# Queries and keys turned by crossbar DMA transposes in a macaron block's attention

## The reference

```python
x = x + 0.5 * ffn(layernorm(x)); x = x + attn(layernorm(x)); x = x + 0.5 * ffn(layernorm(x))

def attn(x):                                   # B, T, C = 8, 512, 128; H, D = 16, 64
    q, k, v = [(x @ W).reshape(B, T, H, D) for W in (Wq, Wk, Wv)]
    q, k = rmsnorm(q, q_rms_w), rmsnorm(k, k_rms_w)        # over D, times a weight for each channel
    gate = softplus(einsum('bthd,hd->bht', k, u_n) / sqrt(D))
    bias = -dist * omega_eff[h] * gate[b, h, j]            # dist = max(i - j, 0), -inf above the diagonal
    attn = softmax(einsum('bihd,bjhd->bhij', q, k) / sqrt(D) + bias)
    return einsum('bhij,bjhd->bihd', attn, v).reshape(B, T, H * D) @ Wproj
```

## Time and profile before

| | us |
|---|---|
| median of 3 runs (lowest, highest) | 913.05 (911.69, 913.4) |
| the profiled execution | 911.52 |
| its span, first to last instruction | 909.7 |
| one round in the middle of it | 102.9 |

### The profile page before, as it was taken

How to read it: one execution, slowest core, us unless ns; L and a number is a source line. 1 busy time by engine, 2 the same in 40 slices (tenths; PEclk the granted TensorE clock), 3 DMA queues, 4 the chain that set the end, 5 groups by cost and what they waited for, 6 DMA issues and landing times.

```text
span 909.7 us, 26061 instructions
## 1 busy us (share of the span) xinstructions
PE 836.1 (92%) x10168; PEld 614.0 (67%) x10168; DVE 691.9 (76%) x1724; ACT 640.0 (70%) x1384; POOL 593.9 (65%) x708
## 2 busy tenths in 40 slices
PE   4648898999999999999999999999999999999984
PEld 2234766578677676777677776777677776777773
DVE  7648776888879887788868888788868888688432
ACT  4645758776877769776877769776877769784633
POOL 3632667577678667687578667687478667686662
PEclk8778999999999999999999999999999999999997
DMA  7033321534051600524052600624042600605000
GB/s 198 4 70 83 84 59 29 114 69 87 2 123 43 142 1 23 133 62 94 2 111 47 152 1 11 146 60 96 2 103 52 151 6 1 153 23 122 3 14 12
DMA packets 28962, 61.18 MB, mean 67 GB/s; under 512 B 5398, under 2 KB 15848, under 8 KB 28776
## 3 DMA queue, kind: packets, MB, share of 16 engines
q1 hardware_dynamic: 28840, 59.52, 29.1%
HBM read 5.29 MB, written 2.10 MB: 8 GB/s over the span
## 4 chain that ended last, share of the span: by engine, by line
PE 69%; DVE 12%; ACT 9%; POOL 5%; issue 4%; SPq 1%; DMA 0%; POOLq 0%; ACTq 0%; DVEq 0%
PE ps L749 12%; PE ps L751 11%; PE ps L750 11%; PE ps L845 6%; PE ps L860 6%; PE ps L887 6%; PE ps L888 6%; DVE negm L1117 4%; POOL pt_l L573 3%; PE ps L775 3%; PE ps L757 3%; PE ps L889 2%; PE ps L861 2%; ACT sq L667 2%; ACT qkn L668 2%
## 5 line engine op out<-in xcount | busy, mean ns | idle before, releaser
L573 POOL TENSOR_TENSOR pt_l<-pt 128x512 f16<-128x512 f32 (+1 forms) x384 | 332.7, 899 | 139.1 <-ACT pt L725 138.5
L1117 DVE TENSOR_REDUCE negm<-ps 128x1 f16<-128x512 f32 (+3 forms) x512 | 213.1, 485 | 22.9 <-PE ps L861 22.4
L725 ACT ACTIVATE pt<-ps 128x512 f32<-128x512 f32 (+1 forms) x384 | 177.5, 533 | 54.8 <-PE ps L889 42.8
L591 POOL TENSOR_TENSOR qkn<-qkn,rs 128x512 f32<-128x512 f32 x128 | 132.6, 1067 | 85.4 <-ACT rs L678 85.4
L887 PE MATMUL ps<-q,k 128*128 128x512 f16 (+3 forms) x512 | 146.7, 299 | 1.1 <-ACT pt L725 1.1
L888 PE MATMUL ps<-q,k 128*128 128x512 f16 (+3 forms) x512 | 146.5, 299 | 0.0
L749 PE MATMUL ps<-v_buf,pt 128*128 128x65 f16 x1280 | 129.6, 194 | 8.6 <-DVE ytok L1135 6.7
L860 PE MATMUL ps<-k,q 96*128 96x512 f16 (+3 forms) x512 | 121.7, 307 | 14.4 <-DMA k<-gtt 7.5
L749 PEld LDWEIGHTS ps<-v_buf,pt 128*128 128x128 bf16 x1280 | 118.1, 98 | 18.0 <-issue 13.0
L750 PE MATMUL ps<-v_buf,pt 128*128 128x65 f16 x1280 | 129.8, 193 | 0.0
L751 PE MATMUL ps<-v_buf,pt_l 128*128 128x65 f16 x1280 | 129.6, 193 | 0.0
(11 more groups left out here) (174 smaller groups left out, 2076.1 us busy)
## 6 DMA issues: line engine op xcount, KB each, us to landing
q<-qkn SPq DMA_DIRECT2D x96, 256.0 KB, 4.9
k<-qkn SPq DMA_DIRECT2D x96, 256.0 KB, 5.7
x_in<-in_L_attn_x SPq DMA_DIRECT2D x8, 256.0 KB, 3.1
out<-x_out SPq DMA_DIRECT2D x8, 256.0 KB, 6.4
k<-q SPq DMA_DIRECT2D x1, 1024.0 KB, 10.4
k<-gtt SPq DMA_DIRECT2D x64, 8.0 KB
sq<-in_L_ffn_W SPq DMA_DIRECT2D x2, 256.0 KB
q<-in_L_attn_Wq SPq DMA_DIRECT2D x1, 512.0 KB, 4.7
```

Of the source, the lines that this page charges most:

```text
L573: g.tensor_tensor(pt_l[:, h % 2, c], pt[:, h % 2, c], pt_h[:, h % 2, c], ALU.subtract).then_inc(s_pt_l, 1)
L591: g.tensor_tensor(qk, qk, r.unsqueeze(3).broadcast_to([P, HH // 2, 2, D]), ALU.mult).then_inc(s_qkn, 1)
L725: a.activation(pt[:, h % 2, c], ps[:, j, 0:width], ACT.Exp).then_inc(s_exp, 1)
L1117: ins = d.tensor_reduce(negm[:, ib, row(h):row(h) + 1], part.bank(s, i)[:, col:col + (ib + 1) * P], AX.X, ALU.max, negate=True)
```

## The change

Queries and keys stay with tokens on partitions through the norm and the split. ACT copies them from PSUM into `qkf` (two buffers by token block), POOL multiplies both by the inverse root and the queries once more by a row `qkw` = query weight x key weight / 8, so that the keys need no weight. In the step `tr` (half, token block), which replaces `t`, ACT writes the high part into `qkt`, DVE the low part beside it (both read SBUF), and SP issues two DMA transposes of 128 x 1024 16-bit elements, `qkt` to `k2` and to `q2`. `rows` is then two copies of 64 partitions x 8 heads x 512 tokens, from `q2` and `k2` to `q1` and `k1`, and the four rows of gates. A half thus has 8 transposes of 256 KB and 2 copies of 512 KB. Heads lie in `q1`, `k1`, `q2`, `k2` in their own order, and `row()` and its like are gone. The weights are first loaded into `pt`, `pt_l` and `q2` in place of `q2` and `k2`. The tables `PART` are written anew.

```diff
 PART = {
...
     "body": [
...
-        ("s", 9, THIS), ("gl", 0, NEXT), ("t", 0, NEXT), ("t", 1, NEXT), ("gate", 0, NEXT), ("pv", 8, THIS),
-        ("t", 2, NEXT), ("t", 3, NEXT),
-        ("s", 10, THIS), ("gr", 0, NEXT), ("pl", 9, THIS), ("pl", 10, THIS), ("rows", 0, NEXT), ("yt", 3, THIS),
...
+        ("s", 15, THIS), ("tr", 1, 0, NEXT), ("tr", 1, 1, NEXT), ("qk", 1, 2, NEXT), ("pl", 14, THIS),
+        ("qkn", 1, 2, NEXT), ("a", 5, NEXT), ("qk", 1, 3, NEXT), ("a", 6, NEXT), ("a", 7, NEXT), ("pv", 14, THIS),
+        ("nm", 0, NEXT), ("qkn", 1, 3, NEXT), ("pl", 15, THIS), ("tr", 1, 2, NEXT), ("wp", 2, THIS), ("gl", 1, NEXT),
+        ("tr", 1, 3, NEXT), ("yt", 6, THIS), ("gate", 1, NEXT), ("v", 0, 3, NEXT),
...
-UNITS = {"m": 2, "h": 4, "out": 1, "qk": 2, "gl": 1, "gr": 1, "t": 2, "a": 3, "nm": 1, "v": 1, "yt": 1, "wp": 1}
+UNITS = {"m": 2, "h": 4, "out": 1, "qk": 2, "gl": 1, "gr": 1, "a": 3, "nm": 1, "v": 1, "yt": 1, "wp": 1}
...
-        qkn = sb("qkn", [P, 2, 2, HH // 2, T // 2])
+        qkf = sb("qkf", [P, 2, 2, HH * D])
+        qkt = sb("qkt", [P, 2, 2, HH, 2, D], F16)
...
+            def turn_operands(part, s, b, hf, t):
+
+                blk = (b * 2 + hf) * TB + t
+                if b > 0 and t == 0:
+                    sp.wait_ge(s_s_ps, ((b - 1) * H + (hf + 1) * HH) * 3)
+                for n, (j, dst) in enumerate(((1, k2), (0, q2))):
+                    sp.wait_ge(s_lo, blk * 2 + n + 1)
+                    sp.dma_start_transpose(dst[:, hf * HH:(hf + 1) * HH, t * P:(t + 1) * P],
+                                           qkt[:, t % 2, j, :, :, :].rearrange("p h a n -> p (h a n)")).then_inc(s_turned[t % 2], 16)
+
             def place_operands(part, s, b, hf):
 
-                def place(dst, j, lo, done):
-                    for n in range(2):
-                        sp.dma_start(dst[:, (2 * hf + n) * HH // 2:(2 * hf + n + 1) * HH // 2, :],
-                                     qkn16[n * D:(n + 1) * D, j, lo, :, :]).then_inc(done, 16)
-
-                sp.wait_ge(s_hi, b * H + (hf + 1) * HH)
-                place(q1[0:D, :, :], 0, 0, s_grow)
-                place(k1[0:D, :, :], 1, 0, s_grow)
+                hs = slice(hf * HH, (hf + 1) * HH)
+                for i in range(2):
+                    sp.wait_ge(s_turned[i], (b * 2 + hf + 1) * TB * 16)
+                sp.dma_start(q1[0:D, hs, :], q2[0:D, hs, :]).then_inc(s_grow, 16)
+                sp.dma_start(k1[0:D, hs, :], k2[D:P, hs, :]).then_inc(s_grow, 16)
                 part.taken(sp, ("gr", *s[1:]))
                 for r in range(4):
-                    sp.dma_start(k1[GROW + r:GROW + r + 1, hf * HH:(hf + 1) * HH, :],
-                                 gtt[r * HH:(r + 1) * HH, :]).then_inc(s_grow, 16)
-                place(q2[0:D, :, :], 0, 0, s_dup)
-                place(k2[D:P, :, :], 1, 0, s_dup)
-                part.taken(sp, ("t", 4 * hf + 3, s[-1]), 1)
-                place(q2[D:P, :, :], 0, 1, s_low)
-                place(k2[0:D, :, :], 1, 1, s_low)
+                    sp.dma_start(k1[GROW + r:GROW + r + 1, hs, :], gtt[r * HH:(r + 1) * HH, :]).then_inc(s_grow, 16)
...
             def over_rms(part, s, b, hf, t):
-                pool.wait_ge(s_rs, (b * 2 + hf) * TB + t + 1)
-                for j in range(2):
-                    qk = qkn[:, j, t // 2, :, (t % 2) * P:(t % 2 + 1) * P].rearrange("p i (h n) -> p i h n", n=D)
-                    r = in_rows(rs[:, t, j * HH:(j + 1) * HH])
-                    g.tensor_tensor(qk, qk, r.unsqueeze(3).broadcast_to([P, HH // 2, 2, D]), ALU.mult).then_inc(s_qkn, 1)
+                blk = (b * 2 + hf) * TB + t
+                pool.wait_ge(s_rs, blk + 1)
+                heads = [qkf[:, t % 2, j, :].rearrange("p (h n) -> p h n", n=D) for j in range(2)]
+                r = [rs[:, t, j * HH:(j + 1) * HH].unsqueeze(2).broadcast_to([P, HH, D]) for j in range(2)]
+                g.tensor_tensor(heads[0], heads[0], r[0], ALU.mult).then_inc(s_qn, 1)
+                g.tensor_tensor(heads[1], heads[1], r[1], ALU.mult).then_inc(s_kn, 1)
...
+                g.tensor_tensor(heads[0], heads[0], qkw[:, :].unsqueeze(1).broadcast_to([P, HH, D]), ALU.mult).then_inc(s_qnw, 1)
...
+                    if blk >= 2:
+                        act.wait_ge(s_lo, (blk - 2) * 2 + 2 - j)
+                    part.taken_by(a.activation(qkf[:, t % 2, j, :], part.bank(s, j), ACT.Copy, scale=1.0 / QKV_UP), s, j)
+
+            def hi_parts(part, s, b, hf, t):
+
+                blk = (b * 2 + hf) * TB + t
+                if blk >= 2:
+                    act.wait_ge(s_turned[t % 2], (blk // 2) * 32)
+                for j in (1, 0):
+                    act.wait_ge(s_kn if j else s_qnw, blk + 1)
+                    a.activation(qkt[:, t % 2, j, :, j, :], qkf[:, t % 2, j, :].rearrange("p (h n) -> p h n", n=D),
+                                 ACT.Copy).then_inc(s_hi, 1)
...
-            def turn_heads(part, s, b, p):
-
-                pe.wait_ge(s_qkn, (b * 2 + p // 4 + 1) * TB * 2)
-                for j in range(2):
-                    part.room(pe, s, j)
-                    for t in range(TB):
-                        mm = pe.transpose(part.bank(s, j)[:, t * P:(t + 1) * P],
-                                          qkn[:, j, t // 2, p % 4, (t % 2) * P:(t % 2 + 1) * P], ident[:, :])
-                    part.filled_by(mm, s, j)
...
+            def lo_parts(part, s, b, hf, t):
+                blk = (b * 2 + hf) * TB + t
+                for n, j in enumerate((1, 0)):
+                    dve.wait_ge(s_hi, blk * 2 + n + 1)
+                    d.tensor_tensor(qkt[:, t % 2, j, :, 1 - j, :], qkf[:, t % 2, j, :].rearrange("p (h n) -> p h n", n=D),
+                                    qkt[:, t % 2, j, :, j, :], ALU.subtract).then_inc(s_lo, 1)
```

More of the change, by code:

```diff
@@ L140, in units_of @@
     return UNITS.get(s[0], 0)
-def units(part):
-    return sum(units_of(s) for s in PART[part])
 def slopes_of(heads):
@@ L348, in macaron @@
         s_out = sem("s_out")
-        s_dup = sem("s_dup")
-        s_low = sem("s_low")
+        s_turned = [sem(f"s_turned{i}") for i in range(2)]
         s_grow = sem("s_grow")
@@ L378, in macaron @@
         s_hi = sem("s_hi")
+        s_lo = sem("s_lo")
+        s_qkw = sem("s_qkw")
         s_s_ps = sem("s_s_ps")
@@ L700, in gate_softplus @@
                 a.activation(lgl[:, :, :], lge[:, :, :], ACT.Ln, bias=1.0).then_inc(s_lgl, 1)
-            def hi_parts(part, s, b, p):
-                if b == 0 and p == 0:
-                    act.wait_ge(s_prepared, 1)
-                for j, w in enumerate((qws, kws)):
-                    part.full(act, s, j)
-                    a.activation(qkn16[:, j, 0, p % 4, :], part.bank(s, j), ACT.Identity, scale=w[:, :]).then_inc(s_hi, 1)
             def v_hi(part, s, b, j, t):
```

328 lines of the change are left out of this document (146 added, 182 removed).

## The result

| | before | after |
|---|---|---|
| median of 4 runs each (lowest, highest), us | 913.04 (911.69, 913.4) | 989.05 (987.96, 994.29) |
| span of the profiled execution, us | 909.7 | 992.4 |
| a round in the middle, us | 102.9 | 116.0 |

The ratio is 1.084, with a 95% interval of 1.080 to 1.089. The forecast was 882 us, and its range ended at 940: wrong in sign, and the time lies above that of every rival too (974 at most).

A forecast was written before the change was run, and what follows sets the result against it. PE was taken as the bound, busy 101.1 of 102.9 us a round. Seven rounds 4.9 us shorter and a lead 3 us longer gave 911.5 - 7 x 4.9 + 3 = 880.2, so 882 us at the median; range 857 to 940.

The forecast's parts named there:

- coupling cost: In a round, PE waiting through the two-buffer chain of ACT, DVE and POOL: 3.1 us, between 0 and 8.
- The gain on PE: In a round, PE's turns (line 845) go: 8.0 us less, from readings of 8.8 and 7.2, leaving 93.1 us of work.
- The sum's "7 x": Seven rounds between 104.7 and 825 us, each taken as 4.9 us shorter (98.0 instead of 102.9).
- DVE's low parts: On DVE, 16 a round at 0.69 us by length plus 0.5 waiting beside POOL; DVE at 90.8 us a round.
- POOL's sum: POOL from 72.5 to 89.0 us a round: 8 more operations at 1.06 us, and waits of 16 x 0.5.
- ACT: ACT's 16 high parts a round at 0.63 instead of 0.70 us: 78.7 to 77.6 us a round.
- The lead: The stage up to 104.7 us, bound by dependences: 3 us longer, between -2 and +8.
- The tail: The last 84.7 us, where PE is busy 67.5: they keep their chain, 0 us.
- D: Time between transposes on the queue, bounds 1.04 and 5.7 us; taken as 1.4 to 2.4, hidden at a round's end, no charge.
- transposes too slow: Rival at a round's end: transposes delay the maxima row and ACT, decisive from 3.5 us each; 940 us, chance 0.21.
- The rival with DVE and POOL as the bound: In rounds, each low part waits a whole POOL operation, 1.06 us: rounds of 101.6 us, 907 us, chance 0.16.
- the two pages: Trainium skill on DMA transposes: one gives 1309 ns per 128 x 128 (10.5 us here), the other says fast as regular DMAs.

The follow-up runs named there:

- e15: Kernel before, with an extra DVE maximum over 128 x 192 of a constant SBUF tile ahead of each low part; 937.4 us (1.028).
- e6: Kernel before, with a third POOL operation for every block, a multiplication of the queries by ones; 971.1 us (1.063).
- e16: e15 plus a POOL multiplication of 128 x 64 ahead of each of its 16 multiplications by the rms in a round; 945.7 us (1.036).
- e9: e3 with four buffers of `qkf` instead of two; 915.1 us (1.002).
- e10: Changed kernel with four buffers of `qkf` instead of two; 989.7 us (1.085).
- e1: Changed kernel, DVE's low parts replaced by an operation reading one SBUF row of zeros, subtraction left out; 920.1 us (1.009).
- e3: e1 with POOL's multiplication by the query weights also left out; 916.4 us (1.004).
- e8: Kernel before with the changes of both e6 and e7; 1004.1 us (1.099).
- e14: e10 with two `tr` steps of each half moved behind the next `qk`; 976.0 us (1.070).
- e4: Changed kernel with four `tr` steps moved: two of the first half set apart, two of the second up to three heads earlier; 997.5 us (1.093).
- e17: e3 with each transpose replaced by a plain DMA copy of the same tile, turn left out, blocks scaled by 0.01; 903.3 us (0.990).
- e7: Kernel before, DVE's low parts reading a constant SBUF tile in place of PSUM, true low parts left out; 953.8 us (1.044).
- e12: Changed kernel with the low parts made on POOL instead of DVE; 1049.8 us (1.150).
- e18: Changed kernel with each transpose replaced by a plain DMA copy, turn left out, blocks scaled by 0.01; 986.8 us (1.080).

## Why the prediction was wrong, point by point

- **The step that failed** is the coupling cost, "I take 3.1 us a round", with 8 as its upper end. Measured is 116.0 - 94.9 = 21.1 us: 12.7 of idle time (14.5 less 1.8), 6.2 of lower clock behind the waits, and 2.2 that PE's work was underrated. The bound was wrong in kind: it was said that the cost can't be more than PE gives up. The rule used was busy time against the round ("no other engine is over PE"). The runs show that idle time of a helper was no slack where it was needed: DVE's 4.0 us in e15 were paid as 3.9 with DVE at 82% of the round, POOL's 9.7 us in e6 as 6.5, and only e16's 3.9 on POOL, on top of e15, as 0.6.
- **What the coupling rests on** was wrong too: not the two buffers (e9, e10: other waits take their place). The timelines point to the fixed order, in which four low parts or six POOL operations in a row stand ahead of what PE needs. That the added work makes the loss is shown (e1 to e3, e6 to e8); that it does so by these runs of operations is read from the waits of one round, and of the reorderings e14 got back 14 of 76 us, e4 none.
- **The gain on PE** is the other half of the error. Its size first: 101.1 less 95.3 is 5.8 us, not 8.0; less than either reading of the earlier trace rows, so that more of the turns lay under their neighbours than 64 x 0.11 lets one think. "1.8 us a round is all that any reordering could give; only less work on PE shortens a round" holds for the old kernel, but taking PE's work away does not shorten a round in the middle either: e17 has 95.3 us of work, and 103.1 us a round. Only the first interval got shorter. The sum's "7 x" took all seven for alike. It seems that PE was full, and at the same time the chain through ACT, POOL and DVE about as long. What of it is the new order and what would stay in any order is not settled: no version of the old order without PE's turns was run.
- **DVE's low parts**: 1.19 predicted, 1.237 measured, from 0.67 to 1.75 with a median of 1.37. The mean is right, and so is what it rests on the earlier trace rows: e1's operation with one input took 0.68. By the Trainium skill ("SBUF — State Buffer", Who interferes with whom) DVE and GpSimd share a port pair, and that is an exclusive lock. The runs agree as far as lengths go: e7's POOL grew by 4.0 us a round with no work added. They show, with e16, at most 8 us of loss in the whole kernel beyond these lengths.
- **POOL's sum**, 89.0 against 89.2, was right by two errors. The third operation takes 1.27 us undisturbed (e12, e6), not 1.06, and 1.40 in the changed kernel: 11.2 us in place of 8.5. The waits of 16 x 0.5 = 8 us were less, spread over more: 0.08 on each of 48 low parts of exponentials (0.98 against 0.90) and 0.03 to 0.12 on the other two, some 5.3.
- **ACT**: 77.6 against 78.8. **The lead**: +3 against +4.3. **The tail**: 0 against +1.5. All near.
- **The transposes**: issued every 1.2 to 1.8 us where the low parts allow it, so D near 1.4, "hidden", right; e18 has them at 2 us of 76. The rival that came closest in time (940 to 974, "transposes too slow") names a mechanism that isn't there.
- **The rival with DVE and POOL as the bound** had the right engines, and the wrong price: it let them cost only once one of them had no idle time left (101.6 us a round).
- **What decides between the two pages** that the prediction set against each other: a transpose of 128 x 1024 landed in 3.3 us, a plain copy of the same bytes into the same place in 3.0 and 3.1 (e18) or 3.1 and 3.7 (e17). So the Trainium skill's "Advanced Engine Details and Errata", X-Bar Transpose (TRN2), agrees with the runs, and the estimate of 10.5 us from the figure in "VectorE: DVE Perf Modes", The three transpose paths, does not.

No version here beats the kernel before with the whole computation done. The best of the changed line that does it is e14, 976.0 us.
